# A four-layer model on one core: values on the head sums' banks in a causal front, an early activation table, head-sum masks built in the router, and the norm of two chunks inside a local attention loop with the bias additions behind it

## The reference, cut to what matters

```python
x = x + _L1_ffn_ref(_layernorm(x), ...)    # top 2 of 8 experts
x = x + _L2_attn_ref(_layernorm(x), ...)   # causal, 16 heads of 8
x = x + _L2_ffn_ref(_layernorm(x), ...)    # two inner layers, below

def _L2_attn_ref(x, Wq, Wk, Wv, Wo, q_scale, k_scale):
    q, k, v = silu(x @ Wq.T), silu(x @ Wk.T), silu(x @ Wv.T)   # then 16 heads
    r_q, r_k = norm(q, axis=-1), norm(k, axis=-1)              # of each head's 8 values
    scores = (q / (r_q + EPS)) @ (k / (r_k + EPS)).T * (r_q * sq) * (r_k * sk)
    return (softmax(tril(scores)) @ v).reshape(B, N, D) @ Wo.T

def _layer(x, wqkv, qs, ksc, wo, lg, lb, w1, b1, w2, b2):      # twice, DEPTH = 2
    ...                                     # q, k, v of 8 heads of 64, rotary
    x = x + local_attention(q, k, v) @ wo   # windows of 64 tokens, one back
    h = shift_token(x)                      # second half of the columns from the token before
    h = (h - h.mean(-1)) / sqrt(h.var(-1) + 1e-05) * lg + lb
    a, g = split(h @ w1 + b1)               # two times 341
    return x + (a * gelu(g)) @ w2 + b2
```

## Time and profile before

| | |
|---|---|
| time, median of 3 runs | 2606.03 us (2598.0 to 2606.3) |
| the profiled execution: time, span | 2600.83 us, 2599.1 us |
| its mean granted TensorE clock | 0.900 |
| busy share of the span: PE, DVE, ACT, POOL | 83%, 72%, 58%, 29% |

### The profile page before, as it was taken

One profiled execution on the slowest core, in us unless ns is written; L12 is line 12 of the kernel. 1 busy time (PEld: TensorE's weight loads), 2 busy tenths in 40 slices (PEclk: granted clock), 3 DMA queues, 4 the chain that ended last, 5 costly groups with the idle time before them and its releaser, 6 DMA issues. The chain is left out here.

```text
span 2599.1 us, 57534 instructions
## 1 busy us (share of the span) xinstructions
PE 2166.1 (83%) x22021; PEld 1129.0 (43%) x22050; DVE 1873.2 (72%) x2868; ACT 1517.7 (58%) x3185; POOL 755.3 (29%) x1331
## 2 busy tenths in 40 slices
PE   5988567799999999966867999998679887876688
PEld 3764344133333333225742444444347546645533
DVE  4646766999999999625467887875586496657577
ACT  3553553488888888852433777777359357542321
POOL 4880001000000000003730222222386286504356
PEclk8997777699999999987975999999889998987789
DMA  3320003321211212000113222221110010000000
GB/s 101 79 58 0 12 1 96 79 55 29 55 46 38 55 31 52 4 20 22 52 47 106 62 75 62 75 61 25 44 36 16 17 30 6 20 25 3 1 1 17
DMA packets 79724, 104.64 MB, mean 40 GB/s; under 512 B 35287, under 2 KB 53881, under 8 KB 79454
## 3 DMA queue, kind: packets, MB, share of 16 engines
q1 hardware_dynamic: 67102, 90.22, 13.2%
q10 hardware_dynamic: 9856, 5.64, 1.0%
q0 software_dynamic: 2496, 5.12, 0.7%
HBM read 80.53 MB, written 14.09 MB: 36 GB/s over the span
## 5 line engine op out<-in xcount | busy, mean ns | idle before, releaser
L978 DVE TENSOR_REDUCE l1a_core_mpart<-l1a_core_psA 128x1 f32<-128x1024 f32 x512 | 601.0, 1220 | 38.5 <-PE l1a_core_psA L890 27.0
L960 ACT ACTIVATE l1a_core_prob<-l1a_core_psB 128x512 f32<-128x512 f32 x1024 | 552.0, 596 | 102.0 <-PE l1a_core_psB L905 91.1
L1322 ACT ACTIVATE l2a_core_prob<-l2a_core_psB 128x384 f32<-128x384 f32 (+3 forms) x656 | 303.5, 526 | 133.4 <-PE l2a_core_psB L1260 129.8
L1347 DVE TENSOR_REDUCE l2a_core_mpart<-l2a_core_psA 128x1 f32<-128x1024 f32 (+4 forms) x352 | 291.1, 879 | 40.5 <-PE l2a_core_psA L1242 38.7
L917 PE MATMUL l1a_core_psV<-l1a_core_prob,l1a_core_vh 128*32 128x512 f32 x2048 | 266.5, 596 | 0.2 <-ACT l1a_core_prob L960 0.2
L905 PE MATMUL l1a_core_psB<-l1a_core_qh,l1a_core_kh 75*32 75x512 bf16 x2560 | 196.2, 383 | 0.5 <-ACT l1a_core_prob L960 0.5
L1276 PE MATMUL l2a_core_psV<-l2a_core_prob,l2a_core_vh 128*32 128x256 f32 (+3 forms) x1856 | 168.0, 419 | 0.4
L1187 POOL TENSOR_SCALAR_AFFINE_SELECT l2a_core_prob<-l2a_core_prob 128x128 f32<-128x128 f32 x256 | 73.9, 293 | 314.4 <-ACT l2a_core_prob L1322 311.1
L850 POOL CAST l1a_core_mb<-l1a_core_negm 128x16 bf16<-128x16 f32 x16 | 3.1, 197 | 472.5 <-PE l1a_core_psA L890 408.6
L1260 PE MATMUL l2a_core_psB<-l2a_core_qh,l2a_core_kh 75*32 75x512 bf16 (+3 forms) x1720 | 134.8, 338 | 0.9 <-ACT l2a_core_prob L1322 0.7
L905 PE MATMUL l1a_core_psB<-l1a_first_qh,l1a_first_kh 75*32 75x512 bf16 x1536 | 119.3, 388 | 4.8 <-ACT l1a_core_prob L960 4.8
(11 more groups left out here) (740 smaller groups left out, 4562.7 us busy)
## 6 DMA issues: line engine op xcount, KB each, us to landing
l2f_tab<-in_rotary SPq DMA_DIRECT2D x32, 128.0 KB, 2.1
l0a_core_qh<-qparts SPq DMA_DIRECT2D x36, 96.0 KB
l0a_core_kh<-kparts SPq DMA_DIRECT2D x36, 96.0 KB
l1a_core_qa<-qparts SPq DMA_DIRECT2D x32, 96.0 KB
l1a_core_ka<-kparts SPq DMA_DIRECT2D x32, 96.0 KB
l2a_core_qa<-qparts SPq DMA_DIRECT2D x32, 96.0 KB
l2a_core_ka<-kparts SPq DMA_DIRECT2D x32, 96.0 KB
l1a_core_qh<-qparts SPq DMA_DIRECT2D x30, 96.0 KB
```

Source lines behind the costliest of these rows:

```text
L960: nc.scalar.activation(prob[u % (2 * PER_KB)][:], psB[u % 3][:], ACT.Exp, scale=scale).then_inc(b_exped, 1)
L978: nc.vector.tensor_reduce(mpart[:, n // 2, n % 2:n % 2 + 1], psA[i % 2][:], AX.X, ALU.max).then_inc(a_freed, 1)
L1322: nc.scalar.activation(prob[n % RING][:, 0:cols], psB[n % 3][:, 0:cols], ACT.Exp, scale=scale).then_inc(b_exped, 1)
L1347: ins = nc.vector.tensor_reduce(mpart[:, place, part:part + 1], psA[i % 2][:, lo * P:hi * P], AX.X, ALU.max)
```

## The change

Five things are rewritten, and the rest of the program is as it was.

1. In the front, values 0 and 1 go to `psN` before `spread_out(1)`, values 2 and 3 behind it; ACT copies values 0 and 1 out earlier in its list, and a one-element activation at the start of ACT's block comes ahead of its first wait. PE no longer waits for all values before `pick_rows`.
2. `HeadSums.build` stands in the router's POOL program, ahead of the first gather, and no longer at the end of the experts.
3. In the attention loop, chunk 0's and 1's `moments`, `power` and `normalise` stand in the iterations n = 9, 12 and n = 13, 16 (`power` behind POOL's copies of t = 10 and 14). The shift of chunk 3 moves to the start of the feed-forward stage.
4. In the feed-forward stage, `moments` and `normalise` of chunks 2 and 3 stand around units 0, 1 and 2; POOL does both powers first and the bias additions when all rows are normalised; PE turns chunk 1 behind the first unit; a one-element Gelu comes first on ACT; PE's end reads `down(3)`, `turn(6)`, `turn(7)`.
5. In inner layer 1 the last chunk's norm takes a root on ACT and a reciprocal on DVE in place of POOL's power.

```diff
 def attention_front
-                values(psF)
+                values(psN, range(0, 2))
                 spread_out(1)
-                pe.wait_ge(v_ready, NC)
+                values(psN, range(2, 4))
...
+            if head_scales:
+                nc.scalar.activation(start[:], g.ident[0:1, 0:1], func)
...
             cast_first(0, 0)
+            value(0, psN)
+            value(1, psN)
             cast_first(0, 1)
-            value(0, psF)
             cast_second(0, 0)
-            value(1, psF)
             cast_second(0, 1)
-            value(2, psF)
-            value(3, psF)
+            value(2, psN)
+            value(3, psN)
 def router
                 sparse.build(pool)
+                on_pool(pool)
                 sparse.gather_first(pool)
 def l1_experts
-            on_pool(pool)
 def local_attention
-            for c in range(NC):
+            for c in range(NC - 1):
                 sp.wait_ge(added, 4 * (c + 1))
                 shifted.shift(sp, c)
...
-            pool.wait_ge(back_ready, 2 * NT)
-            for c in range(NC - 1):
-                shifted.power(pool, c)
+                if t in (10, 14):
+                    pool.wait_ge(back_ready, 2 * (t + 1))
+                    shifted.power(pool, (t - 10) // 4)
...
-                if 0 <= n - NT < NC - 1:
-                    shifted.moments(dve, n - NT)
-                if 0 < n - NT < NC:
-                    shifted.normalise(dve, n - NT - 1)
+                if n in (9, 13):
+                    shifted.moments(dve, (n - 9) // 4)
+                if n in (12, 16):
+                    shifted.normalise(dve, (n - 12) // 4)
 def local_ffn
+        @block.sync
+        def _(sp):
+            shifted.shift(sp, NC - 1)
...
             pool.wait_ge(loaded, W * (l + 1))
+            shifted.power(pool, NC - 2)
+            shifted.power(pool, NC - 1)
+            pool.wait_ge(shifted.normed, NT)
...
-                if c == 0:
-                    shifted.power(pool, NC - 1)
...
-            turn(1)
...
-                    if k == 0 and 1 <= c < NC - 1:
+                    if k == 0 and c < NC - 1:
                         turn(c + 1)
...
+            down(NC - 1)
             turn(2 * NC - 2)
-            down(NC - 1)
             turn(2 * NC - 1)
...
+            nc.scalar.activation(first[:], g.ident[0:1, 0:1], ACT.Gelu)
             out(0)
-            out(1)
...
-                if c == 0 and k == 1:
-                    shifted.moments(dve, NC - 1)
-                if c == 0 and k == 2:
-                    shifted.normalise(dve, NC - 1)
+                if n < 2:
+                    shifted.moments(dve, NC - 2 + n)
+                if 1 <= n < 3:
+                    shifted.normalise(dve, NC - 3 + n)
...
-                norm.normalise_by_power(dve, NC - 1)
+                norm.normalise_by_root(dve, NC - 1)
```

More of the change, by code:

```diff
@@ L406, in power, with normalise_by_root @@
         self.nc.gpsimd.tensor_tensor(r, r, self.g.minus_half[:], ALU.pow).then_inc(self.rstd_ready, 1)
+    def normalise_by_root(self, dve, c):
+        dve.wait_ge(self.std_ready, c + 1)
+        self.nc.vector.reciprocal(self.rstd[:, 4 * c:4 * c + 4], self.std[:, 4 * c:4 * c + 4]).then_inc(self.rstd_ready, 1)
+        self.normalise_by_power(dve, c)
     def normalise_by_power(self, dve, c):
@@ L1401, in attention_front @@
         nrm, dn = st.sb("nrm", [P, 2, SEG]), st.sb("dn", [P, 2, SEG])
-        gather = head_sums(g)
+        gather, start = head_sums(g), st.sb("start", [1, 1])
         psN = [st.ps(f"psN{i}") for i in range(2)]
@@ L1443, in _, with values @@
                 nc.tensor.matmul(out, w[:, which, :], x, start=True, stop=True).then_inc(projected, 1)
-            def values(banks):
-                for t in range(NT):
+            def values(banks, chunks=range(NC)):
+                for t in range(4 * chunks[0], 4 * chunks[-1] + 4):
                     c = t // 4
@@ L1450, in values @@
                         pe.wait_ge(v_ready, c - 1)
+                    elif t % 4 == 0:
+                        pe.wait_ge(norm_ready, c + 1)
                     nc.tensor.matmul(banks[c % len(banks)][:, t % 4 * P:(t % 4 + 1) * P], g.XnT[:, t * P:(t + 1) * P], w[:, 2, :],
@@ L2162, in load, with router @@
             sp.dma_start(dst, src).then_inc(self.loaded, 16)
-def router(nc, g, name, E, weights, parts=None, sparse=None):
+def router(nc, g, name, E, weights, parts=None, sparse=None, on_pool=None):
     st = Stage(nc, name)
@@ L2486, in place, with l1_experts @@
         chain(reduce(self.bias[:], by_part, AX.X, ALU.add))
-def l1_experts(nc, g, ew, norm, on_sync, sparse, on_pool):
+def l1_experts(nc, g, ew, norm, on_sync, sparse):
     E, HID, J, T, K = ew.E, ew.HID, ew.J, sparse.TILES, sparse.K
@@ L2662, in l1_ffn @@
 def l1_ffn(nc, g, a):
-    router(nc, g, "l1r", 8, g.l1_router, sparse=g.l1_sparse)
+    sums = HeadSums(nc, g)
+    router(nc, g, "l1r", 8, g.l1_router, sparse=g.l1_sparse, on_pool=sums.build)
     g.l2_norm = RowNorm(nc, g, "l2a_ln")
@@ L2666, in l1_ffn @@
     g.l2_front = FrontWeights(nc, g, "l2a_w", (a["L2_attn_WqT"], a["L2_attn_WkT"], a["L2_attn_WvT"]), head_scales=scales)
-    sums = HeadSums(nc, g)
-    l1_experts(nc, g, g.l1_experts, g.l2_norm, g.l2_front.load, g.l1_sparse, sums.build)
+    l1_experts(nc, g, g.l1_experts, g.l2_norm, g.l2_front.load, g.l1_sparse)
     g.l2_norm.close(sums)
@@ L4058, in local_ffn @@
     h = [st.sb(f"h{i}", [P, 3, CH]) for i in range(2)]
+    first = st.sb("first", [1, 1])
     psA = [st.ps(f"psA{i}") for i in range(2)]
@@ L4072, in local_ffn @@
     with st.block() as block:
-        if on_sync is not None:
-            @block.sync
-            def _(sp):
+        @block.sync
+        def _(sp):
+            shifted.shift(sp, NC - 1)
+            if on_sync is not None:
                 on_sync(sp)
@@ L4087, in _ @@
                     nc.gpsimd.tensor_tensor(x, x, r, ALU.add).then_inc(based, 1)
-                if c == 0:
-                    shifted.power(pool, NC - 1)
-            for c in range(NC if norm else 0):
+            for c in range(NC - 1 if norm else 0):
                 norm.power(pool, c)
@@ L4175, in _ @@
                     out_next(c - 2)
+            if norm:
+                norm.root(act, NC - 1, NC)
             out_next(NC - 2)
```

## The result

Over ten runs of each kernel the median went from 2603.91 to 2589.39 us; the ratio is 0.9949, 95% interval 0.9939 to 0.9960. The medians differ by 14.5 us, and the ratio stands for 13; the forecast was a median of 2587 (2577 to 2598). The profiled execution has a span of 2586.2 us, 12.9 less than before.

What follows compares the result with a forecast made beforehand. No engine bounds the whole (PE busy 83%, DVE 72%); waits at each touched place do. Terms sum to -16.5 us, giving 2584.3 from the profiled 2600.83 or 2589.5 from the median; forecast 2587, range 2577 to 2598.

Steps and rivals of the forecast that it cites:

- front: Layer 2's attention front: keys' `spread_out` directly after values 0 and 1 ends key scaling earlier; -5.2 us, bounds -4.6 to -7.
- early Silu table: Front of layer 2's attention: table load moves into ACT's first wait, but PE is the cover; 0 us.
- masks out of the experts' end: Experts' end: DVE's slow addition beside the last select returns to 0.692 us; -1.6 us, least gain -1.3.
- masks into the router: Router: POOL's selects delay DVE's comparisons by one and three quarters of a select; +3.5 us, bounds +0.2 and +4.5.
- last shift: End of each inner layer's attention loop: stage no longer waits for SP's last shift; -4.25 us each, bounds -4.0 to -4.4.
- norm in the loop: Each inner layer's attention loop: `normalise` beside POOL's scaling delays maxima 1.5, power delays scaling 0.25; +1.8 us, bounds 1.1 to 2.5.
- start of the feed-forward stage: Both inner layers: POOL's additions no longer beside `normalise(3)`, chunk 2's norm added; -0.7 and -1.9 us.
- last stage's end: Inner layer 1's feed-forward end: `down(3)` starts earlier, -4.7 us; root and reciprocal replace power, -1.0; together -5.7.
- the two bases of the prediction: Whole kernel: profiled execution of 2600.83 us gives 2584.3, the median of the runs shown gives 2589.5; 2587 lies midway.
- so one or two of the four rows get through: Attention loop: `normalise` starts at most 0.15 us ahead of POOL's scaling, remaining rows wait 1.90; maxima 1.5 us late at n = 12.
- the rival of the dear ends: Router and both loops: DVE blocked wherever POOL works, feed-forward gain hidden by buffers; gains 6 to 11 us, about 2595; chance 0.16.
- The clock, booked as a rival: Feed-forward start: without the pause PE's clock holds, up to 2.2 us more for each layer, about 2579; chance 0.15.

Runs made afterwards that it cites:

- after: The changed kernel, with all five rewrites, against the kernel before: median 2589.39 us from 2603.91, ratio 0.9949.
- after's second profile: The changed kernel itself, run and profiled a second time, against the kernel before: ratio 0.9949, interval 0.9930 to 0.9969.
- a free loop: Changed kernel with power and normalise of chunks 0 and 1 moved behind the loop's last POOL work: loops 87.03 and 87.08 us, ratio to before 0.9929.
- bias ahead: Changed kernel with POOL's powers behind its chunk 0 additions, the other additions beside the norm: feed-forward stages 41.81 and 47.22 us, one run.

## Why the prediction was right

The range held, and so did the mechanisms of the front, the masks, the last shift and the last stage's end. In the profile of after each term but the loop's came out within about 0.5 us (the sum takes the -2.4 of the experts' stage):

| term | forecast | measured |
|---|---|---|
| front | -5.2 | -5.7 |
| early Silu table | 0 | 0 |
| masks out of the experts' end | -1.6 | -1.7 there; -1.3 to -2.4 of the stage |
| masks into the router | +3.5 | +3.3 |
| last shift | -4.25, twice | -4.28 and -4.30 |
| norm in the loop | +1.8, twice | +3.1 and +4.7 |
| start of the feed-forward stage | -0.7 and -1.9 | -0.65 and -1.7 |
| last stage's end | -5.7 | -6.0 |
| sum | -16.5 | -14.0 |

That closeness is partly luck. In after's second profile the same stages sum to -10.5: the front gives -5.1, the experts -1.3, layer 0's feed-forward stage +1.0, and the others are as above. And 2587 was a choice midway between the two bases of the prediction; the sum itself was 2 to 4 us too large, against 12.9 us in the spans and 14.5 in the medians.

**The loop** is the mis-sized term, outside its bounds of 1.1 to 2.5. The step was "so one or two of the four rows get through": it took the power to cost only a later scaling. But `normalise` waits for that power, which ends 0.4 us behind the reciprocal, and so POOL issues first: none gets through, and the iteration is 2.17 longer. With the power one iteration earlier the loops lose 1.87 and 1.78 against the 87.0 of a free loop, the forecast 1.8. The second miss is "At n = 16 there is no maxima behind it": `lay_p(15)` is, and it lost 0.8 us. The rest, 1.6 in layer 1, goes with PE's clock after the longer iteration (0.69). So of the rival of the dear ends the loops' part came, and went beyond the 2.5 that it had.

**The router** lost 1.7 us in each of two comparisons, those of 1.94 and 1.91 us, which came up beside a running select and ended with it. The rule of the Trainium skill, "SBUF — State Buffer", section "Who interferes with whom", that whoever issues first holds the shared port pair for the whole instruction, agrees with these rows. The +4.2 worked out by that rule was too much, since DVE got in between two selects. The forecast's +3.5 was a choice between bounds of +0.2 and +4.5, and its closeness is luck too.

**The start of the feed-forward stage** came out by sums of other things than forecast. The Gelu table was booked at 0 because PE's turns and first unit would cover it. They did before; now the load stands ahead of the copy on which the first unit waits, and costs 0.6 us per stage. The clock, booked as a rival, did hold at this place in after's profile in both layers, in its second one in layer 1 alone; it is worth 1.5 to 1.7 each, where the rival had up to 2.2. The reason that the term names, POOL's additions beside `normalise`, explains about 1.3 us in layer 1 and nothing in layer 0 (bias ahead). So layer 0's -0.65 is luck: at the lower clock of the second profile the stage is 1.0 us longer than before.

## What to carry to other kernels

Before work is moved beside another engine's, look which of the two will be issued first, and count what it waits for: here the same four instructions took 1.1 us in the tail, 3.0 ahead of POOL's scaling and 3.4 behind it, and everything queued behind them paid. Whether a gap in an engine's timeline is free depends on the instruction: beside the same scaling the moments took what they take alone, and `normalise` took three times as long. Where several small gains are made at once, a ledger by stage shows what the total cannot, since edits worth 1 to 5 us by their stage were not clear of noise in the time. But set the granted clock of each stage beside it: a stage of the same code differed by 1.5 to 1.7 us with it, as much as most of these edits are worth.
